# Attention scores through four single PSUM banks, row maxima through one double and one single bank

## The chip, the cores and the metric

The kernel runs on one core of a Trainium2 chip. The metric is the device time of one execution in microseconds (us). The kernel before took 948.18 us, the median of three runs (947.07 to 959.93). The profiled execution took 946.91 us, of which 945.1 us are its span.

## The reference

A transformer block with conditioning, on x of 2 x 1024 x 288 in float32. What the change touches is the attention of 16 heads of 18 columns:

```python
h = _modulate(_ln(x), sh_msa, sc_msa)
qkv = (h @ w_qkv + b_qkv).reshape(B, N, 3, nh, hd).transpose(2, 0, 3, 1, 4)
q, k, v = (qkv[0], qkv[1], qkv[2])
attn = jax.nn.softmax(jnp.einsum('bhqd,bhkd->bhqk', q, k) * hd ** (-0.5), axis=-1)
o = jnp.einsum('bhqk,bhkd->bhqd', attn, v).transpose(0, 2, 1, 3).reshape(B, N, C)
o = o @ w_proj + b_proj
x = x + g_msa[:, None, :] * o
```

Ahead of it stand the layer norm and the projections, behind it a second layer norm, a choice of two of four experts for each token, and the experts' two matrix products.

## The kernel before

The program has four stages: a setup (to about 81 us of the span), the attention (to about 523 us), a stage between (output projection, second norm, gate, loading of the experts' weights), and the experts (from about 631 us).

The attention works on 8 groups (`GG`), each of 4 heads (`GH`) of one batch. A group has 16 steps: two halves of 512 queries, each with 8 tiles of 128 keys. A step makes, for each of the 4 heads, the scores of 128 keys against 512 queries (`scores`, L1165), their exponentials on ScalarE (`exponential`, L1033), and adds their product with v to a bank `o_ps` (`values`, L1179). The values of a step are issued one step later.

The maximum of each query's scores is needed ahead of the exponentials. So every score is computed twice. Beside the steps of one group TensorE computes, for a later half, the scores with queries along the partitions (`maxima`, L1132), and VectorE reduces them to row maxima (L1064). Such a product of 128 queries by 512 keys is called a block. A half of a group (a "turn") has 32 blocks. When a turn's blocks are done, VectorE reduces them to one row each (`rowmax`, L1068), TensorE transposes those ("rows", L1139), VectorE splits the result in two parts (L1078, L1080), and two DMAs put them in the operand of the later scores. When a half's values are done, ScalarE copies `o_ps` to `o_sb` (L1040), TensorE transposes that ("out", L1145), and VectorE normalises it (L1087, L1091).

Maxima, rows and out are *items* with one running number n. Item n uses the buffer `m_ps[n % 2]`; a max item of before fills both banks of it with two blocks, and one reduction of 1024 elements per partition reads them. Before TensorE starts item n it waits for `max_free` n + 1, a count that begins at 2 and that VectorE raises once for each item it has finished. So item n starts when item n-2 is finished. In `MaxPlan` it is written which items are issued in which step: 48 blocks (`AHEAD`) ahead of the first step (the *lead*), then 4 a step (`RATE`), until all 512 are done in the middle of the eighth group.

The order on TensorE in a step is fixed: the scores of heads 0 and 1; the step's first item; the values of the step before; the scores of heads 2 and 3; its second item; in the steps 1, 4, 7 and 10 of the first six groups half of a projection for a later group (`project`, L441, 7 matmuls); any further items; the rest of the projection.

Scores and projections share a ring of single banks `s_ps` (`S_BANKS`): the k-th user takes bank k modulo the number of banks, and waits until ScalarE has read the one that many places back (`slot_free`). Two heads' operands lie on partitions 0 to 55 and 64 to 119, so that two matmuls next to each other, of an even and an odd head, use different halves of the array's rows. Blocks too alternate between an even and an odd head.

All eight PSUM banks are in use: 3 in the ring, 4 for the maxima, 1 for `o_ps`.

Of the kernel before, what the change touches and what calls it, by code (L numbers as in the profile page):

```python
# [6 lines left out]
ALU = mybir.AluOpType  # L7
ACT = mybir.ActivationFunctionType
AX = mybir.AxisListType
# [6 lines left out]
P = 128  # L16
# [10 lines left out]
HALF = N // 2  # L27
# [25 lines left out]
def f32(ap):  # L53

    return ap.bitcast(F32)
# [38 lines left out]
def build_kernel(nc, x, cond, w_adaln, b_adaln, w_qkv, b_qkv, w_proj, b_proj, w_gate, w1, b1, w2, b2, out):  # L94
# [20 lines left out]
    with outer:  # L115
# [20 lines left out]
        with before_experts:  # L136
            mod_late = far(before_experts, "mod_late", [P, B, 3 * C])
            outputs_in = OutputTiles(far, sem, before_experts, o_dram)
            setup_and_attention = ExitStack()
            with setup_and_attention:  # L140
                v_aug = sb(setup_and_attention, "v_aug", [P, NT, NH, HA])

                wqk = (sb(setup_and_attention, "wqk_raw", [P, 3, 2, GC]),
                       sb(setup_and_attention, "wqk_hi", [P, 3, 2, GH, HP], F32R),
                       sb(setup_and_attention, "wqk_lo", [P, 2, 2, GH, HP], F32R),
                       sb(setup_and_attention, "bqk", [P, GG, 2]),
                       sem(setup_and_attention, "w_ld"), sem(setup_and_attention, "w_split"),
                       sem(setup_and_attention, "bias_ld"))
                heads = HeadParts(nc, sb, sem, setup_and_attention, x_hi, x_lo, wqk)
                late.stage_in(heads.parts)  # L150
                setup(nc, sb, pb, sem, xt, cond, w_adaln, b_adaln, w_qkv, b_qkv, x_hi, x_lo, mod_late, g_mlp, ident,
                      half_neg, v_aug, wqk, heads, outputs_in.tiles)
                attention(nc, sb, pb, sem, w_qkv, ident, v_aug, wqk, heads, o_dram, late, outputs_in)
            gate_bank = pb(outer, "gate_bank", [P, 512])
            between(nc, sb, pb, sem, xt, ot, outputs_in, mod_late, ident, half_neg, xn_dram, gate_bank, logits, late, x1_st)
# [640 lines left out]
PAIRS = GH // 2  # L796
BLOCKS = 2 * GH * QT
PAIR_BLOCKS = 2
S_BANKS = 3
AHEAD = 48  # L800
RATE = 4
PROJ_AT = (1, 4, 7, 10)
# [9 lines left out]
def proj_item(g, u):  # L812

    return u if g == 1 else score_item(g - 2, PROJ_AT[u], GH - 1) + 1


class MaxPlan:
# [22 lines left out]

    def maxima(self, items, upto):
        while self.block < min(upto, 2 * GG * BLOCKS):
            n = PAIR_BLOCKS
            if self.block + n > upto:
                break
            items.append((self.count, "max", self.block // BLOCKS, self.block % BLOCKS, n))
            self.block, self.count = self.block + n, self.count + 1
# [7 lines left out]
def attention(nc, sb, pb, sem, w_qkv, ident, v_aug, wqk, heads, o_dram, late, outputs_in):  # L855
# [7 lines left out]
    ctx = ExitStack()  # L863
    with ctx:
# [4 lines left out]
        negmax = sb(ctx, "negmax", [P, 2, BLOCKS])  # L869
# [8 lines left out]
        late.tail_buffers(sb, ctx)  # L878

        s_ps = [pb(ctx, f"s_ps{i}", [P, HALF]) for i in range(S_BANKS)]  # L880
        m_ps = [pb(ctx, f"m_ps{i}", [P, 2, HALF]) for i in range(2)]
        o_ps = pb(ctx, "o_ps", [P, HALF])

        zero_ok = sem(ctx, "zero_ok")
# [15 lines left out]
        def max_bank(n):  # L900

            return m_ps[n % 2][:, 0]
# [76 lines left out]
        def _(pool):  # L979
# [8 lines left out]
            def parts(g, u):  # L988
                half, a = u // 2, u % 2
                hi, lo = ((heads.Q_HI, heads.Q_LO), (heads.K_HI, heads.K_LO))[a]  # L990
                pool.wait_ge(slot_free, S_BANKS + proj_item(g, u) + 1)
                if u == 0:
# [24 lines left out]
        def _(act):  # L1017

            act.sem_inc(slot_free, S_BANKS)

            def project(g, u):
                k = proj_item(g, u)
                act.wait_ge(slot_mm, k + 1)
                act.wait_ge(parts_ok, heads.parts_count(g, u) - 4)
                nc.scalar.activation(heads.proj_f[:, u % 2], s_ps[k % S_BANKS][:], ACT.Identity,  # L1025
                                     bias=wqk[3][:, g, u % 2:u % 2 + 1]).then_inc(slot_free, 1)

            def exponential(g, st, h):
                k = score_item(g, st, h)
                act.wait_ge(slot_mm, k + 1)  # L1030
                if h == 0:
                    act.wait_ge(pv_free, 16 * g + st + 1)
                nc.scalar.activation(probs[:, st % 2, h], s_ps[k % S_BANKS][:], ACT.Exp, scale=SCALE)\  # L1033
                  .then_inc(slot_free, 1)
# [21 lines left out]
        @block.vector  # L1056
        def _(dve):
            nc.vector.memset(o_ps[:], 0.0).then_inc(zero_ok, 1)
            dve.sem_inc(max_free, 2)

            def maxima(n, turn, first, count):
                half = turn % 2
                dve.wait_ge(max_mm, n + 1)
                nc.vector.tensor_reduce(negmax[:, half, first:first + count], m_ps[n % 2][:], AX.X, ALU.max, negate=True)\  # L1064
                  .then_inc(max_free, 1)
                if first + count == BLOCKS:
                    dve.wait_ge(max_free, 2 + n + 1)
                    nc.vector.tensor_reduce(rowmax[:, half].rearrange("p (h b) -> p b h", h=2),  # L1068
                                            negmax[:, half].rearrange("p (b k h) -> p b h k", k=2, h=2), AX.X, ALU.min)\
                      .then_inc(rowmax_ok, 1)  # L1070

            def rows(n, turn):
                g, half = turn // 2, turn % 2
                bank = max_bank(n)
                dve.wait_ge(max_mm, n + 1)
                if g >= 1:
                    dve.wait_ge(rows_ld[half], 64 * g)
                nc.vector.tensor_copy(rows_hi[:, half], bank[0:GH * QT, 0:P]).then_inc(rows_step, 1)  # L1078
                dve.wait_ge(rows_step, turn + 1)
                nc.vector.tensor_tensor(rows_lo[:, half], bank[0:GH * QT, 0:P], f32(rows_hi[:, half]),  # L1080
                                        ALU.subtract).then_inc(max_free, 1)

            def normalise(n, turn):
                g, half = turn // 2, turn % 2
                o = max_bank(n).rearrange("p (t c) -> p t c", c=HP)
                dve.wait_ge(max_mm, n + 1)
                nc.vector.reciprocal(rsum[:, half], o[:, :, HD]).then_inc(rsum_ok, 1)  # L1087
                dve.wait_ge(rsum_ok, turn + 1)
                if g >= 1:
                    dve.wait_ge(out_st[half], 16 * g)  # L1090
                nc.vector.tensor_tensor(o_norm[:, half], o[:, :, 0:HD],  # L1091
                                        rsum[:, half].unsqueeze(2).broadcast_to([P, QT * GH, HD]),
                                        ALU.mult).then_inc(max_free, 1)

            def item(n, kind, turn, first, count):
                if kind == "max":
                    maxima(n, turn, first, count)
                elif kind == "rows":
                    rows(n, turn)
                else:  # L1100
                    normalise(n, turn)

            for items in (plan.lead, *plan.steps, plan.last):
                for it in items:
                    item(*it)

        @block.tensor
        def _(pe):
            pe.sem_inc(pv_free, 2)

            def project(g, u, some):
                k = proj_item(g, u)
                if some.start == 0:
                    if u == 0:
                        pe.wait_ge(w_split, 4 * (g + 1))
                    pe.wait_ge(slot_free, k + 1)
                mm = heads.products(g, u % 2, u // 2, s_ps[k % S_BANKS][:], some)
                if some.stop == len(PRODUCTS):
# [30 lines left out]
            def item(n, kind, turn, first, count):  # L1149
                if kind == "max":  # L1150
                    maxima(n, turn, first, count)
                elif kind == "rows":
                    rows(n, turn)
                else:
                    outputs(n, turn)
# [892 lines left out]
```

## Time and profile before

| what | value |
|---|---|
| median of 3 runs | 948.18 us |
| profiled execution, and its span | 946.91 us, 945.1 us |
| TensorE busy / VectorE busy / ScalarE busy | 827.9 / 568.5 / 476.4 us |
| attention, first to last values | 114.49 to about 523 us |
| lead, first block to first scores | 82.40 to 110.89 us |

A line of the page or of a table of groups gives the program line, the engine, the operation, output and inputs with their shapes, and how many; then the busy time and the mean of one, and the idle time of the engine just ahead with what ended it. In a timeline the first number is the start in us from the span's start, the second the length of the merged instructions, and in brackets stands the idle time ahead. The ends of matmuls are modelled, so the starts are what to read.

### The profile page before, as it was taken

What the parts mean: (1) busy time and instruction counts of PE and PEld (TensorE: products, weight loads), DVE (VectorE), ACT (ScalarE), POOL (GpSimd) and SP (SyncE); (2) the same over time, 40 slices, a digit from 0 to 9 for tenths busy, and PEclk for the clock granted to TensorE, in tenths of its full rate; (3) what the DMA queues carried; (4) which work ended last, traced back from release to release, by engine and by line L of the source; (5) the groups of instructions that cost most, each with busy time, mean ns of one, the idle gap of its engine ahead of it and who ended that gap; (6) DMA issues with size and microseconds to landing.
All of it is one profiled execution on the core that took longest, in us unless ns stands there. A gap on an engine that the chain in (4) does not pass through costs nothing. (4 is left out here: it accounts for less than half of the span.)

```text
span 945.1 us, 15242 instructions
## 1 busy us (share of the span) xinstructions
PE 827.9 (88%) x5111; PEld 554.2 (59%) x5111; DVE 568.5 (60%) x994; ACT 476.4 (50%) x975; POOL 341.3 (36%) x348
## 2 busy tenths in 40 slices
PE   4886799999999999999988885369999999999995
PEld 3683333333333333333322563259999999999995
DVE  3765878777787778778860493825455434434432
ACT  0540267666676676667777364344334333333331
POOL 6534221131212222110422298066555444344332
PEclk9896799999999999999999795579999999999998
DMA  8021120424131221203222394134332222222221
GB/s 219 10 57 28 40 49 20 88 83 92 22 85 23 63 51 34 65 8 84 78 55 66 110 285 153 53 109 113 81 64 36 39 46 37 38 45 38 38 37 20
DMA packets 56384, 62.98 MB, mean 67 GB/s; under 512 B 24184, under 2 KB 50662, under 8 KB 55736
## 3 DMA queue, kind: packets, MB, share of 16 engines
q1 hardware_dynamic: 47304, 49.30, 20.1%
q0 software_dynamic: 8400, 12.12, 7.7%
q8 instruction: 46, 0.75, 0.3%
q10 hardware_dynamic: 608, 0.59, 0.2%
q14 instruction: 26, 0.21, 0.1%
HBM read 33.87 MB, written 15.73 MB: 52 GB/s over the span
## 5 line engine op out<-in xcount | busy, mean ns | idle before, releaser
L1064 DVE TENSOR_REDUCE negmax<-m_ps 128x2 f32<-128x1024 f32 x256 | 306.5, 1221 | 73.9 <-PE m_ps L1132 73.7
L1033 ACT ACTIVATE probs<-s_ps 128x512 f32<-128x512 f32 x512 | 269.8, 602 | 105.3 <-PE s_ps L1165 105.2
L1165 PE MATMUL s_ps<-stack 56*128 56x512 f32 x512 | 161.5, 476 | 21.2 <-ACT probs L1033 21.2
L1165 PEld LDWEIGHTS s_ps<-stack 56*128 56x128 f32 x512 | 65.5, 185 | 181.8 <-ACT probs L1033 154.6
L1132 PE MATMUL m_ps<-stack 54*128 54x512 f32 x512 | 136.6, 452 | 15.2 <-DVE negmax L1064 7.9
L1179 PE MATMUL o_ps<-probs,v_aug 128*19 128x512 f32 x1024 | 136.4, 605 | 6.3 <-ACT o_sb L1040 5.1
L2013 PE MATMUL gate_bank<-weights,ht_hi 128*128 x630 | 127.1, 296 | 0.4 <-DVE ht_lo L1909 0.4
L1989 PE MATMUL h_ps<-weights,xt_hi 128*128 x525 | 115.3, 350 | 4.6 <-DVE xt_hi L1902 4.6
L995 POOL CAST parts<-proj_f 128x512 fp32r<-128x512 f32 x28 | 17.1, 610 | 261.9 <-ACT proj_f L1025 129.3
L1687 POOL DMA_INDIRECT out<-res,ido x35 | 56.9, 1624 | 140.5 <-DVE res L1931 140.5
L1735 ACT CAST ht_hi<-ht_ps 128x384 fp32r<-128x384 f32 x105 | 43.6, 488 | 119.7 <-PE ht_ps L2000 119.7
L2013 PEld LDWEIGHTS gate_bank<-weights,ht_hi 128*128 128x128 f32 x630 | 101.4, 189 | 0.6 <-issue 0.6
L1989 PEld LDWEIGHTS h_ps<-weights,xt_hi 128*128 128x128 f32 x525 | 93.9, 193 | 5.2 <-issue 5.2
L2013 PE MATMUL gate_bank<-weights,ht_lo 128*128 x315 | 93.2, 296 | 0.0
L1729 ACT ACTIVATE hid<-h_ps 128x384 f32<-128x384 f32 x105 | 51.5, 492 | 69.5 <-PE h_ps L1989 69.3
L1132 PEld LDWEIGHTS m_ps<-stack 54*128 54x128 f32 x512 | 56.7, 192 | 34.9 <-DVE negmax L1064 15.4
L1931 DVE SCALAR_TENSOR_TENSOR res<-gate_bank,cws,scale 128x288 f32<-128x288 f32 x35 | 18.1, 518 | 93.5 <-PE gate_bank L2013 91.6
L1901 DVE TENSOR_TENSOR xt_lo<-tx_ps,xt_hi 128x256 fp32r<-128x256 f32 x35 | 14.9, 425 | 82.6 <-issue 58.6
L2013 PEld LDWEIGHTS gate_bank<-weights,ht_lo 128*128 128x128 f32 x315 | 59.2, 188 | 0.0
L1909 DVE TENSOR_TENSOR ht_lo<-ht_ps,ht_hi 128x384 fp32r<-128x384 f32 x105 | 52.1, 551 | 5.4 <-ACT ht_hi L1735 5.1
L1989 PE MATMUL h_ps<-weights,xt_lo 128*128 x210 | 54.8, 342 | 0.0
L1025 ACT ACTIVATE proj_f<-s_ps,bqk 128x512 f32<-128x512 f32 x28 | 19.3, 688 | 63.7 <-PE s_ps L441 63.7
(213 smaller groups left out, 1117.9 us busy)
## 6 DMA issues: line engine op xcount, KB each, us to landing
stack<-parts SPq DMA_DIRECT2D x96, 144.0 KB
w_raw<-in_L_cond_w SPq DMA_DIRECT2D x9, 432.0 KB
w_raw<-in_L_cond_w SPq DMA_DIRECT2D x9, 384.0 KB
xn_scratch<-h SPq DMA_DIRECT2D x16, 192.0 KB, 3.7
x_in<-in_x SPq DMA_DIRECT2D x4, 576.0 KB, 8.6
o_scratch<-o_norm SPq DMA_DIRECT2D x16, 144.0 KB, 2.4
o_in<-o_scratch SPq DMA_DIRECT2D x16, 144.0 KB, 2.6
xr<-in_x SPq DMA_DIRECT2D x16, 144.0 KB, 3.0
```

Source lines behind the costliest of these rows:

```text
L1025: nc.scalar.activation(heads.proj_f[:, u % 2], s_ps[k % S_BANKS][:], ACT.Identity, bias=wqk[3][:, g, u % 2:u % 2 + 1]).then_inc(slot_free, 1)
L1033: nc.scalar.activation(probs[:, st % 2, h], s_ps[k % S_BANKS][:], ACT.Exp, scale=SCALE)\
L1064: nc.vector.tensor_reduce(negmax[:, half, first:first + count], m_ps[n % 2][:], AX.X, ALU.max, negate=True)\
L1132: mm = nc.tensor.matmul(m_ps[n % 2][:, i], stack[s][r, j, 0, half, qt * P:(qt + 1) * P], stack[s][r, j, 1, kh], start=True, stop=True)
L1165: nc.tensor.matmul(s_ps[k % S_BANKS][:], stack[s][r, j, 1, kt // QT, (kt % QT) * P:(kt % QT + 1) * P], stack[s][r, j, 0, half], start=True ...
L1179: mm = nc.tensor.matmul(o_ps[h * HP:h * HP + HA], v_aug[:, tile, (g % NG) * GH + h], probs[:, st % 2, h], start=(kt == 0), stop=(kt == KT ...
L1687: nc.gpsimd.indirect_dma_start(out_rows, bass.IndirectOffsetOnAxis(ap=ido[:, j:j + 1], axis=0), res[j % 2][:], None, compute_op=ALU.add).t ...
L1729: nc.scalar.activation(hid[:, c * UPC:(c + 1) * UPC], h_ps[c][:, 0:UPC], ACT.Gelu_apprx_tanh)\
L1735: nc.scalar.copy(ht_hi[:, 3 * c:3 * (c + 1)], ht_ps[c][:]).then_inc(hthi_ok, 1)
L1909: nc.vector.tensor_tensor(ht_lo[:, s], ht_ps[c][:], f32(ht_hi[:, s]), ALU.subtract)\
L1989: mm = nc.tensor.matmul(h_ps[c][:, 0:UPC], (xt_hi, xt_lo)[xs][:, xk], words(j, (3 * ws + wk) * H + c * UPC, UPC), start=(i == 0), stop=(i ...
L2013: mm = nc.tensor.matmul(y_ps[:, 0:C], hs[:, ht], words(j, 5 * H + (HT * ws + ht) * C, C), start=False, stop=(ht == HT - 1 and i == 2))
```

## The change

The ring `s_ps` has four banks. The second buffer of the maxima has one bank. A max item with an even number has two blocks, one with an odd number has one, and the last block of a turn goes alone where only one is left. Everything else (the number of blocks in each step as far as they fit, the order within a step, the matmuls) is written as it was.

```diff
-S_BANKS = 3
+S_BANKS = 4
@@ def maxima(self, items, upto):
         while self.block < min(upto, 2 * GG * BLOCKS):
-            n = PAIR_BLOCKS
+            room = BLOCKS - self.block % BLOCKS
+            n = PAIR_BLOCKS if self.count % 2 == 0 and room >= PAIR_BLOCKS else 1
             if self.block + n > upto:
                 break
@@ def attention
-        m_ps = [pb(ctx, f"m_ps{i}", [P, 2, HALF]) for i in range(2)]
+        m_ps = [pb(ctx, f"m_ps{i}", [P, 2 - i, HALF]) for i in range(2)]
@@ VectorE, def maxima
-                nc.vector.tensor_reduce(negmax[:, half, first:first + count], m_ps[n % 2][:], AX.X, ALU.max, negate=True)\
+                nc.vector.tensor_reduce(negmax[:, half, first:first + count], m_ps[n % 2][:, 0:count], AX.X, ALU.max, negate=True)\
```

In all there are 162 double and 188 single max items where there were 256 double ones. D is a double and S a single in what follows.

The first place is TensorE's queue in a plain step (no projection, rows or out). Before, one item stands on each side of the values (L1179), always in the other buffer:

```order
L1179 MATMUL o_ps<-probs,v_aug 19x512 x4
L1165 MATMUL s_ps1<-stack0 128x512
L1165 MATMUL s_ps2<-stack0 128x512
L1132 MATMUL m_ps1<-stack0 128x512 x2
L1165 MATMUL s_ps0<-stack0 128x512
L1165 MATMUL s_ps1<-stack0 128x512
L1132 MATMUL m_ps0<-stack0 128x512 x2
L1179 MATMUL o_ps<-probs,v_aug 19x512 x4
```

Now (the lines are one further down) the steps differ in turn. One such step, and the beginning of the next:

```order
L1180 MATMUL o_ps<-probs,v_aug 19x512 x4
L1166 MATMUL s_ps0<-stack0 128x512
L1166 MATMUL s_ps1<-stack0 128x512
L1133 MATMUL m_ps0<-stack1 128x512 x2
L1133 MATMUL m_ps1<-stack1 128x512
L1166 MATMUL s_ps2<-stack0 128x512
L1166 MATMUL s_ps3<-stack0 128x512
L1133 MATMUL m_ps0<-stack1 128x512 x2
L1180 MATMUL o_ps<-probs,v_aug 19x512 x4
L1166 MATMUL s_ps0<-stack0 128x512
L1166 MATMUL s_ps1<-stack0 128x512
L1133 MATMUL m_ps1<-stack1 128x512
```

Between the two lines L1180 the double buffer `m_ps0` is filled twice with a single in between; before, no buffer was filled twice between two values.

The second place is TensorE's queue around the rows item, in a step with a projection. Before:

```order
L1165 MATMUL s_ps2<-stack0 128x512
L1165 MATMUL s_ps0<-stack0 128x512
L1139 MATMUL m_ps0<-ident,rowmax 16x128
L441 MATMUL s_ps1<-stretch,wqk_hi 128x512 x3
L441 MATMUL s_ps1<-stretch,wqk_lo 128x512
L1132 MATMUL m_ps1<-stack1 128x512 x2
L441 MATMUL s_ps1<-stretch,wqk_lo 128x512
L441 MATMUL s_ps1<-stretch,wqk_hi 128x512 x2
L1165 MATMUL s_ps2<-stack0 128x512
L1165 MATMUL s_ps0<-stack0 128x512
L1132 MATMUL m_ps0<-stack1 128x512 x2
L1179 MATMUL o_ps<-probs,v_aug 19x512 x4
```

Now:

```order
L1166 MATMUL s_ps3<-stack0 128x512
L1166 MATMUL s_ps0<-stack0 128x512
L1140 MATMUL m_ps0<-ident,rowmax 16x128
L441 MATMUL s_ps1<-stretch,wqk_hi 128x512 x3
L441 MATMUL s_ps1<-stretch,wqk_lo 128x512
L1133 MATMUL m_ps1<-stack1 128x512
L1133 MATMUL m_ps0<-stack1 128x512 x2
L441 MATMUL s_ps1<-stretch,wqk_lo 128x512
L441 MATMUL s_ps1<-stretch,wqk_hi 128x512 x2
L1166 MATMUL s_ps2<-stack0 128x512
L1166 MATMUL s_ps3<-stack0 128x512
L1133 MATMUL m_ps1<-stack1 128x512
```

Two items became three: a single stands ahead of the double, and one behind the scores.

The third place is the end of the lead on TensorE, up to the first scores. Before, every item was a double:

```order
L1132 MATMUL m_ps1<-stack0 128x512 x2
L1132 MATMUL m_ps0<-stack0 128x512 x2
L1132 MATMUL m_ps1<-stack0 128x512 x2
L1132 MATMUL m_ps0<-stack0 128x512 x2
L1165 MATMUL s_ps1<-stack0 128x512
L1165 MATMUL s_ps2<-stack0 128x512
```

Now:

```order
L1133 MATMUL m_ps0<-stack0 128x512 x2
L1133 MATMUL m_ps1<-stack0 128x512
L1133 MATMUL m_ps0<-stack0 128x512 x2
L1133 MATMUL m_ps1<-stack0 128x512
L1166 MATMUL s_ps0<-stack0 128x512
L1166 MATMUL s_ps1<-stack0 128x512
```

The lead has 24 doubles before, and now 16 doubles and 15 singles for 47 blocks.

## Rows read from the trace of the kernel before

**Rows 1.** The page, busy time: us (share of the span) x instructions.

```profile
PE 827.9 (88%) x5111; PEld 554.2 (59%) x5111; DVE 568.5 (60%) x994; ACT 476.4 (50%) x975; POOL 341.3 (36%) x348
```

**Rows 2.** The page, costliest groups: the maxima's reductions, the exponentials, the scores' weight loads.

```profile
L1064 DVE TENSOR_REDUCE negmax<-m_ps 128x2 f32<-128x1024 f32 x256 | 306.5, 1221 | 73.9 <-PE m_ps L1132 73.7
L1033 ACT ACTIVATE probs<-s_ps 128x512 f32<-128x512 f32 x512 | 269.8, 602 | 105.3 <-PE s_ps L1165 105.2
L1165 PEld LDWEIGHTS s_ps<-stack 56*128 56x128 f32 x512 | 65.5, 185 | 181.8 <-ACT probs L1033 154.6
```

**Rows 3.** Windows of a group and of three plain steps: busy by engine, PEclk, DMA, GB/s.

```profile
220.53:273.55 53.02, 50.05 (x294) 19.82 (x295) 41.14 (x43) 36.85 (x71) 10.95 (x14) 1.00 0.24 52
261.83:270.33 8.50, 7.85 (x51) 2.75 (x49) 7.62 (x7) 6.20 (x13) 0.28 (x1) 1.00 0.25 55
```

**Rows 4.** Timeline of TensorE, one plain step.

```profile
212.63 0.50 PE L1165 MATMUL s_ps<-stack 56*128 56x512 f32 x2
212.96 0.39 PE L1132 MATMUL m_ps<-stack 54*128 54x512 f32 x2
213.20 0.39 PE L1165 MATMUL s_ps<-stack 56*128 56x512 f32 x1
213.81 0.50 PE L1165 MATMUL s_ps<-stack 56*128 56x512 f32 x1 [0.23 <-ACT probs L1033]
213.81 0.73 PE L1132 MATMUL m_ps<-stack 54*128 54x512 f32 x2
214.47 1.05 PE L1179 MATMUL o_ps<-probs,v_aug 128*19 128x512 f32 x8
215.46 0.50 PE L1165 MATMUL s_ps<-stack 56*128 56x512 f32 x2
```

**Rows 5.** Timelines of ScalarE and VectorE, the same step.

```profile
213.16 2.06 ACT L1033 ACTIVATE probs<-s_ps 128x512 f32<-128x512 f32 x4 [0.76 <-PE s_ps L1165]
...
213.40 2.40 DVE L1064 TENSOR_REDUCE negmax<-m_ps 128x2 f32<-128x1024 f32 x2 [0.43 <-PE m_ps L1132]
```

**Rows 6.** Timeline of TensorE, a step without maxima near the attention's end.

```profile
510.10 0.73 PE L1165 MATMUL s_ps<-stack 56*128 56x512 f32 x3
511.28 0.50 PE L1165 MATMUL s_ps<-stack 56*128 56x512 f32 x1 [0.45 <-ACT probs L1033]
511.76 1.05 PE L1179 MATMUL o_ps<-probs,v_aug 128*19 128x512 f32 x8
512.75 0.50 PE L1165 MATMUL s_ps<-stack 56*128 56x512 f32 x2
```

**Rows 7.** Timelines of TensorE and VectorE, an out item and what waits for it.

```profile
227.58 0.50 PE L1132 MATMUL m_ps<-stack 54*128 54x512 f32 x2 [0.18 <-DVE o_norm L1091]
228.01 1.05 PE L1179 MATMUL o_ps<-probs,v_aug 128*19 128x512 f32 x8
...
227.06 0.46 DVE L1091 TENSOR_TENSOR o_norm<-m_ps,rsum 128x288 f32<-128x288 f32 x1
```

**Rows 8.** Timeline of TensorE, starts of values in the third group.

```profile
220.53 1.05 PE L1179 MATMUL o_ps<-probs,v_aug 128*19 128x512 f32 x8 [0.33 <-ACT o_sb L1040]
224.67 1.05 PE L1179 MATMUL o_ps<-probs,v_aug 128*19 128x512 f32 x8
...
230.83 1.05 PE L1179 MATMUL o_ps<-probs,v_aug 128*19 128x512 f32 x8
...
235.38 1.05 PE L1179 MATMUL o_ps<-probs,v_aug 128*19 128x512 f32 x8
...
245.18 1.05 PE L1179 MATMUL o_ps<-probs,v_aug 128*19 128x512 f32 x8
248.40 1.05 PE L1179 MATMUL o_ps<-probs,v_aug 128*19 128x512 f32 x8 [0.33 <-ACT o_sb L1040]
```

**Rows 9.** Timeline of VectorE in the lead.

```profile
93.13 3.49 DVE L1064 TENSOR_REDUCE negmax<-m_ps 128x2 f32<-128x1024 f32 x3 [0.58 <-PE m_ps L1132]
97.24 4.62 DVE L1064 TENSOR_REDUCE negmax<-m_ps 128x2 f32<-128x1024 f32 x4 [0.62 <-PE m_ps L1132]
101.89 0.19 DVE L1068 TENSOR_REDUCE rowmax<-negmax 128x16 f32<-128x32 f32 x1
...
103.36 12.53 DVE L1064 TENSOR_REDUCE negmax<-m_ps 128x2 f32<-128x1024 f32 x11
```

**Rows 10.** Timeline of TensorE in the lead, and its window (columns as in Rows 3).

```profile
102.52 1.55 PE L1132 MATMUL m_ps<-stack 54*128 54x512 f32 x4
...
81.00:114.50 33.50, 24.39 (x82) 12.17 (x81) 26.96 (x26) 5.61 (x10) 9.68 (x12) 0.70 0.10 20
```

## The prediction

> **What bounds the kernel now.** I began with the busy times: TensorE 88% of the span, VectorE 60%, ScalarE 50% [rows 1]. In a group in the middle of the attention, 53.02 us for 16 steps, TensorE is busy 50.05, VectorE 41.14 and ScalarE 36.85 [rows 3]. Modelled matmul ends fill gaps, so the question of who waits for whom goes to the groups: the scores' weight loads sat idle 154.6 us for the exponentials, and the reductions 73.7 us for TensorE [rows 2]. No engine is full; the steps are a loop with two handovers.
>
> The timeline of a plain step [rows 4, 5] shows the loop. It lasts 2.83 us (212.63 to 215.46). The second score of the next pair starts at 213.81, late by a wait for ScalarE: the ring has three banks, and it needs the one whose exponential began at 213.16 and took 0.60 [rows 2]. Behind it in the queue stand a double and the values, which start 0.66 later at 214.47. After the values, 0.98 later, come the next scores. So with three banks the loop is: score to exponential 0.53, exponential 0.60, handover 0.05, score and double 0.66, values 0.98, in sum 2.83.
>
> Where no maxima are left a step takes 2.65 us (510.10 to 512.75) [rows 6]. There the second score still waits for its bank, and the values start at 511.76, 1.66 behind the scores, once two exponentials are done; that part does not depend on the ring. So 2.65 is the floor of a step with any ring.
>
> **The fourth bank.** It takes away the wait at 213.81. A plain step can come down from 2.83 to 2.65, by 0.18, if nothing else is late. TensorE's own work in it is four pairs of 0.33 and the values of 0.98, or 2.3 us [rows 4], so TensorE has room. A step with a projection takes 4.14 (220.53 to 224.67) [rows 8], with the seven matmuls packed and no ring wait in it: nothing is gained there.
>
> **The maxima, plain steps.** The double item has 1.22 us of VectorE [rows 2]. For the single I take the line between that (1024 elements) and the small reduction of 32 elements in 0.19 [rows 9]: 1.03/992 = 1.04 ns per element, so 0.69 us for 512. Behind another of its kind a double starts 1.14 after it (12.53/11) [rows 9], 0.08 before the first ends; so a queued single costs about 0.61. The work per three plain steps is four doubles and four singles, 4 x 1.14 + 4 x 0.61 = 7.0, against 6 x 1.14 = 6.8 before, of 8.5 us. VectorE isn't full by this. What decides is the wait of a double for the double two items back.
>
> From here on 0 is the start of values. The scores come at 0.98, an item behind them at 1.32 (0.98 + 0.34), its reduction 0.44 later (212.96 to 213.40) [rows 4, 5]. A stalled item starts 0.06 after its release (227.52 to 227.58), and values behind a stalled double come 0.43 later (228.01) [rows 7]. Three kinds of step follow each other:
> - A, with D and S behind the values and D ahead of the next: the first D is reduced from 1.76 to 2.98. TensorE reaches the next D at 1.32 + 3 x 0.33 = 2.31, but may start it only at 3.04. Values at 3.47. Before: 2.83, so +0.64.
> - B, with S and D behind and S ahead of the next: S reduced from 1.76 to 2.45, the next S at 2.51, values at 2.84: 0.
> - C, with S behind and D ahead of the next: the D before was done at about 1.3, so values come at the floor, 2.65: -0.18.
> In sum a cycle of three costs 8.96 instead of 8.49. The ring's gain is left in one step of three, and A pays for it several times.
>
> **The other steps.** At a change of half the values also wait for the copy of `o_ps`, and the step has 3.22 (245.18 to 248.40) [rows 8]; two a group are of kind A and go to 3.47: +0.25 each. The out item in a step without projection: its normalisation starts behind one more single, and the double that waits for it starts near 3.2 instead of 2.91; +0.30. Out with a projection: one more array slot of 0.33 less 0.10 of a wait that the new single covers: +0.23. Rows without projection: D waits for the split rows until 2.39, then 0.43, scores 0.34, S 0.33: 3.49 instead of 2.84, +0.65. Rows with projection, 4.55 (230.83 to 235.38) [rows 8]: one more slot, +0.33. The projection in step 7 gets a double in its middle, as the one with rows has (4.55 against 4.14), and one single more: +0.61. Step 1: 0.
>
> For a group with projections: two A 1.28, two at the changes 0.50, three C -0.54, three B 0, out 0.30 and 0.23, rows 0.65 and 0.33, step 7 0.61: +3.36. Six groups: +20.2. The seventh, without projections, has a C more, two outs of 0.30 and two rows of 0.65: +3.0. In the eighth three steps are left: +0.1. Behind them no step has maxima, and they stay at 2.65.
>
> **The lead.** VectorE goes through doubles back to back at 1.14 and sets the time [rows 9]. Now a double can follow the double before only after 1.22 + 0.06 + the way through TensorE. That way is 0.54 at the full clock (the idle 0.58 and 0.62 of rows 9 hold it), and 0.84 at the lower one (102.52 to 103.36) [rows 9, 10], where the mean clock of the lead was 0.70 [rows 10]. So three blocks take 1.82 to 2.12 us instead of 1.5 x 1.14 = 1.71. In the first 32 blocks every second group of three items between projections gets shorter by 0.7, but only 18 blocks instead of 24 are done with the projections, and six more come after them at 0.6 each: about +2.2. The 15 behind the rows, at 2.12 for three, take 10.6 instead of 8 x 1.14 = 9.1: +1.5, and 0.3 for the wait at the join. I take +4; from below 0 (work alone) and from above 7 (all at the lower clock).
>
> At the attention's end all is in series with the stages behind; they keep their length.
>
> **A rule against the rows.** The step's waits show VectorE busy 7.62 of 8.50 us in plain steps [rows 3], with an idle 0.43 at each turn [rows 5]. The Trainium skill, Perfetto Trace Analysis, section Optimizing Scalar/DVE Operations, says that where such an engine isn't saturated but makes bubbles elsewhere, breaking up instructions may let work finish sooner. By that rule the split would pay, and the time would be that of the first rival below. In the rows no bubble of before comes from the length of a reduction outside the lead, so I give the rule little.
>
> A single also uses half of the array's rows with no partner: the last max matmul in 213.81 to 214.47 starts 0.33 after its partner in time [rows 4], as much as a pair. I count a single at 0.33. If it could run beside its neighbour, step 7, rows and outs would be 0.2 to 0.3 cheaper: -1 us a group. The Trainium skill, TensorE: Matmul & The Clock Gate, Part 3, The mechanism, says that weight loads overlap running matmuls only when the row group differs; by it a single between unlike halves could be hidden, and the sum would be some 6 us lower.
>
> **Sum.** 20.2 + 3.0 + 0.1 + 4 = 27 us on the profiled 946.9: 974. The median of the runs is 1.3 above the profiled time: 975. As plain error I see the singles (-6), the lead (-4 to +3), and 0.1 of a microsecond in each A and rows step (5 a group: 4 in all).
>
> **Rivals.**
> 1. *The ring pays, the maxima don't stall* (8%). If the second D of kind A were free when TensorE gets there (at 2.31), all 66 plain steps would drop by 0.18: -12 us, and with the lead 936 to 940, not slower. For it: the wait for ScalarE is the one that the trace names most [rows 2]. Against: it needs the reduction of 1.22 to end 0.7 earlier. The place is the third item of an A step, and it decides from a release at about 2.3.
> 2. *Half and half* (16%): TensorE's stall is partly given back, since the exponentials run ahead in it, or singles are cheap. A at 3.1 and rows at 3.1 give some +1.2 a group: 950 to 962.
> 3. *The clock* (10%). In the lead the granted clock was 0.70 [rows 10] after TensorE had waited, in the steps 1.00 [rows 3]. If the longer waits keep the whole lead and some first steps at 1.2 GHz, the lead costs 6 to 10 more and the first steps too: 982 to 995.
> 4. My forecast (66%): 962 to 984.
>
> Two per cent, about what can be told from no change here, are 19 us: 967. The forecast's part above that is about nine tenths: slower 0.66 x 0.9 + 0.10 = 0.69, same 0.29, faster 0.02. The range from 954 to 986 leaves out the first rival, a part of the second and most of the third.
>
> **What would show it.** In the trace of the changed kernel: plain steps in a cycle of 3.47, 2.84 and 2.65; in the first of them TensorE's double waits for VectorE's reduction by 0.6 to 0.7; no wait of the second score for its bank; a single reduction of 0.69; a group of 56.4 us instead of 53.0; the first scores at about 115 instead of 110.9; steps without maxima at 2.65. If all plain steps take 2.65 to 2.8, the sum is wrong at A; if a single costs less than 0.2 on TensorE, at the projections; if the lead's clock is another, at the lead.

## The result

The changed kernel takes 986.6 us, the median of four runs (982.33 to 990.75), against 947.63 before in the same comparison: a ratio of 1.0379, 95% interval 1.0282 to 1.0476. It is slower. The forecast was 975, and the median lies 0.6 above the upper end of the range; the ratio times the 948.18 that the forecast started from is 984.1, inside it. The profiled execution is the shortest of the four, 982.33 us with a span of 980.5, which is 35.4 longer than before.

The page of the changed kernel, busy times:

```profile
PE 833.1 (85%) x5111; PEld 559.0 (57%) x5111; DVE 575.6 (59%) x1088; ACT 477.5 (49%) x975; POOL 342.1 (35%) x348
```

It answers to [rows 1]: no engine has noticeably more work. The groups of the changed kernel (each reads busy time and mean of one, then the idle time ahead):

```profile
L1133 PE MATMUL m_ps<-stack 54*128 54x512 f32 x512 | 149.4, 458 | 50.2 <-DVE negmax L1065 42.3
...
L1166 PEld LDWEIGHTS s_ps<-stack 56*128 56x128 f32 x512 | 59.7, 191 | 125.9 <-ACT probs L1034 95.9
```

The scores' wait for ScalarE fell from 154.6 us [rows 2] to 95.9, as a fourth bank should do: with the ring back at three banks it is 145.6 (first experiment below). In its place TensorE's max matmuls wait 42.3 us for VectorE's reductions, where they waited 7.9:

```profile
L1132 PE MATMUL m_ps<-stack 54*128 54x512 f32 x512 | 136.6, 452 | 15.2 <-DVE negmax L1064 7.9
```

The groups by shape show the price of the two kinds:

```profile
L1065 DVE TENSOR_REDUCE negmax<-m_ps 128x2 f32<-128x1024 f32 x162 | 197.9, 1222 | 45.5 <-PE m_ps L1133 45.3
L1065 DVE TENSOR_REDUCE negmax<-m_ps 128x1 f32<-128x512 f32 x188 | 129.0, 686 | 53.6 <-PE m_ps L1133 53.6
```

The single takes 0.686 us; the estimate was 0.69.

The timeline of TensorE through three plain steps of the third group, the three kinds in a row:

```profile
276.32 1.05 PE L1180 MATMUL o_ps<-probs,v_aug 128*19 128x512 f32 x8
277.31 0.50 PE L1166 MATMUL s_ps<-stack 56*128 56x512 f32 x2
277.65 0.40 PE L1133 MATMUL m_ps<-stack 54*128 54x512 f32 x2
277.88 0.39 PE L1166 MATMUL s_ps<-stack 56*128 56x512 f32 x1
277.89 0.39 PE L1133 MATMUL m_ps<-stack 54*128 54x512 f32 x1
278.12 0.39 PE L1166 MATMUL s_ps<-stack 56*128 56x512 f32 x1
279.37 0.50 PE L1133 MATMUL m_ps<-stack 54*128 54x512 f32 x2 [0.86 <-DVE negmax L1065]
279.81 1.05 PE L1180 MATMUL o_ps<-probs,v_aug 128*19 128x512 f32 x8
...
282.46 1.05 PE L1180 MATMUL o_ps<-probs,v_aug 128*19 128x512 f32 x8 [0.46 <-ACT probs L1034]
...
284.96 0.50 PE L1133 MATMUL m_ps<-stack 54*128 54x512 f32 x1 [0.31 <-DVE negmax L1065]
285.39 0.63 PE L1180 MATMUL o_ps<-probs,v_aug 128*19 128x512 f32 x4
```

From values to values: 3.49 (kind A), 2.65 (C), 2.93 (B). Before, each had 2.83 [rows 4]. VectorE over the same time:

```profile
278.09 3.05 DVE L1065 TENSOR_REDUCE negmax<-m_ps 128x2 f32<-128x1024 f32 x3 [0.43 <-PE m_ps L1133]
281.56 1.82 DVE L1065 TENSOR_REDUCE negmax<-m_ps 128x1 f32<-128x512 f32 x2 [0.42 <-PE m_ps L1133]
```

The first double begins at 278.09 and takes 1.22, to 279.31; the next double on TensorE starts at 279.37. Its neighbours, both scores, had started by 278.12: with four banks they wait for nothing, and TensorE then stands idle behind a double.

Windows of the changed kernel (columns as in Rows 3): a whole group, the last group's steps around its last rows item, and behind it.

```profile
232.38:288.86 56.48, 50.21 (x296) 20.56 (x294) 42.19 (x55) 36.96 (x72) 10.99 (x14) 1.00 0.22 49
508.51:518.89 10.38, 7.94 (x53) 3.07 (x52) 8.31 (x12) 6.91 (x14) 1.51 (x1) 1.00 0.05 14
518.89:541.53 22.64, 18.35 (x77) 4.52 (x76) 0.56 (x2) 12.18 (x24) 5.79 (x4) 0.53 0.13 41
```

A group takes 56.48 instead of 53.02 [rows 3]; 56.4 was forecast. The third row was not: in the first steps without maxima the granted clock was 0.53 (0.50 from 520.1 to 544.0), and a plain one of them lasts 3.81 us instead of 2.65 [rows 6]. Before, the corresponding stretch ran at the full clock up to 522.0, and at 0.50 for the 1.2 us that were left to the last values:

```profile
489.50:523.00 33.50, 26.79 (x151) 7.59 (x154) 1.27 (x4) 24.29 (x47) 5.81 (x4) 0.98 0.17 50
```

The lead on VectorE goes as worked out, a double and a single in 1.82 and 0.30 idle behind them, 2.12 for three blocks:

```profile
105.43 1.82 DVE L1065 TENSOR_REDUCE negmax<-m_ps 128x2 f32<-128x1024 f32 x2
107.55 1.82 DVE L1065 TENSOR_REDUCE negmax<-m_ps 128x2 f32<-128x1024 f32 x2 [0.29 <-PE m_ps L1133]
```

The 35.4 us of span, by the starts of values: up to the first values 4.4 (118.87 against 114.49); the first group 4.0; the next five 3.5 each, 17.5; the seventh 2.9; the last, to the start of its last matmul of values, 7.0 (50.55 against 43.53); everything behind it -0.4. Below, the length of the last group is taken to the first matmul of its last values: 50.1 here, 42.7 before.

### The profile page after: what moved, and what is told of

Read it like the earlier page. It is cut to its first block and busy times, and to the rows that moved or that the text cites. A ratio compares the mean times of both kernels' runs of the same rounds, so it can differ in the third digit from the quotient of the medians.

```text
span 980.5 us, 15336 instructions
## 1 busy us (share of the span) xinstructions
PE 833.1 (85%) x5111; PEld 559.0 (57%) x5111; DVE 575.6 (59%) x1088; ACT 477.5 (49%) x975; POOL 342.1 (35%) x348
## 5 line engine op out<-in xcount | busy, mean ns | idle before, releaser
L1065 DVE TENSOR_REDUCE negmax<-m_ps 128x2 f32<-128x1024 f32 (+1 forms) x350 | 317.0, 934 | 99.0 <-PE m_ps L1133 98.8
L1133 PE MATMUL m_ps<-stack 54*128 54x512 f32 x512 | 149.4, 458 | 50.2 <-DVE negmax L1065 42.3
L1180 PE MATMUL o_ps<-probs,v_aug 128*19 128x512 f32 x1024 | 141.0, 624 | 21.3 <-ACT probs L1034 20.0
L1166 PE MATMUL s_ps<-stack 56*128 56x512 f32 x512 | 133.5, 472 | 0.0
L1166 PEld LDWEIGHTS s_ps<-stack 56*128 56x128 f32 x512 | 59.7, 191 | 125.9 <-ACT probs L1034 95.9
L1133 PEld LDWEIGHTS m_ps<-stack 54*128 54x128 f32 x512 | 71.0, 192 | 103.5 <-DVE negmax L1065 80.4
L1180 PEld LDWEIGHTS o_ps<-probs,v_aug 128*19 128x19 f32 x1024 | 17.5, 98 | 64.0 <-ACT probs L1034 38.6
```

Source lines behind the costliest of these rows:

```text
L1133: mm = nc.tensor.matmul(m_ps[n % 2][:, i], stack[s][r, j, 0, half, qt * P:(qt + 1) * P], stack[s][r, j, 1, kh], start=True, stop=True)
L1166: nc.tensor.matmul(s_ps[k % S_BANKS][:], stack[s][r, j, 1, kt // QT, (kt % QT) * P:(kt % QT + 1) * P], stack[s][r, j, 0, half], start=True ...
L1180: mm = nc.tensor.matmul(o_ps[h * HP:h * HP + HA], v_aug[:, tile, (g % NG) * GH + h], probs[:, st % 2, h], start=(kt == 0), stop=(kt == KT ...
```

## The experiments

All times are medians, and each ratio is against the kernel before, run beside it on the same chip. The comparisons among variants rest on these ratios and on the traces.

**The ring back to three banks.**

```diff
-S_BANKS = 4
+S_BANKS = 3
```

> The changed kernel with the ring put back to three banks (one PSUM bank is left unused). My theory: the fourth bank only helps the plain steps of the short kind (single behind the values, double ahead of the next), which go from 2.65 back to 2.83 us; the steps of 3.47 and 2.92 keep their length, a group takes 57.0 instead of 56.5, and the kernel is 3 to 5 us slower than the changed one. Rival, the fourth bank is worth its 0.18 in every plain step: over 10 us slower than the changed one.

Measured: 991.9 us, ratio 1.0475 (1.0458 to 1.0493); a group 57.0. Plain steps 3.48, 2.93 and 2.84. The short one on TensorE:

```profile
284.41 1.05 PE L1180 MATMUL o_ps<-probs,v_aug 128*19 128x512 f32 x8
285.39 0.50 PE L1166 MATMUL s_ps<-stack 56*128 56x512 f32 x2
285.73 0.39 PE L1133 MATMUL m_ps<-stack 54*128 54x512 f32 x1
285.97 0.40 PE L1166 MATMUL s_ps<-stack 56*128 56x512 f32 x1
286.58 0.49 PE L1166 MATMUL s_ps<-stack 56*128 56x512 f32 x1 [0.21 <-ACT probs L1034]
286.58 0.72 PE L1133 MATMUL m_ps<-stack 54*128 54x512 f32 x2
287.24 0.63 PE L1180 MATMUL o_ps<-probs,v_aug 128*19 128x512 f32 x4
```

The second score waits again, with a double behind it, as in [rows 4]. At the full clock that is the whole worth of the fourth bank here: 0.18 us in one plain step of three, 0.5 a group. Against the changed kernel the medians differ by 5 us, the two profiled spans by 9.8 (990.3 against 980.5; the changed kernel's was its shortest). Of the 9.8, the first seven groups hold 4.3, the last group 2.9 (53.0 instead of 50.1; at the lower clock a plain step takes 4.05 instead of 3.81), 2.9 stand ahead of the first values, and -0.3 behind the last. The other two kinds did not feel the ring. So the rival falls by the steps in the trace; the times alone would not decide it, since the ratios differ by 0.0096, or 9 us.

**The first item ahead of the scores, in the kernel before.**

```diff
-                    scores(g, st, 0)
-                    for it in items[:1]:
-                        item(*it)
+                    early = t > 0 and all(it[1] == "max" for it in plan.steps[t - 1])
+                    for it in items[:1] if early else []:
+                        item(*it)
+                    scores(g, st, 0)
+                    for it in items[:1] if not early else []:
+                        item(*it)
```

> The kernel before with one edit on TensorE: a step's first max item is issued ahead of its first two scores instead of behind them, except where the step before holds a rows or out item. My theory of the loop (score, two exponentials, values) says that the ring wait is only harmful because a double stands behind it; moved ahead of it, the wait for the bank runs beside the second exponential and a plain step takes 2.65 instead of 2.83 with three banks. Nine steps a group: about 51.4 instead of 53.0, the kernel at 935 to 939. Rival, the fourth bank is what such a step needs: no change, 2.83.

Measured: 940.49 us, ratio 0.994 (0.9923 to 0.9957); a group 51.6. TensorE in a plain step:

```profile
261.22 1.05 PE L1179 MATMUL o_ps<-probs,v_aug 128*19 128x512 f32 x8
262.20 0.50 PE L1165 MATMUL s_ps<-stack 56*128 56x512 f32 x2
262.54 0.69 PE L1132 MATMUL m_ps<-stack 54*128 54x512 f32 x4
263.08 0.81 PE L1165 MATMUL s_ps<-stack 56*128 56x512 f32 x2
263.88 0.62 PE L1179 MATMUL o_ps<-probs,v_aug 128*19 128x512 f32 x4
```

The step takes 2.66 with three banks. The wait for the bank is still there (the fourth score starts at 263.39, 0.05 behind the end of the exponential that held its bank), but no max item stands between it and the values any more. Eight steps a group with 0.17 make the 1.4 us between 53.0 and 51.6; the ninth plain step, the one with rows and no projection, stayed at 2.83. The kernel got less than forecast (935 to 939), for two more reasons that the trace shows: the last group took 45.0 instead of 42.7, because the clock fell there (two steps of 4.05 and 3.81), and the first step after the lead took 6.05 instead of 4.72.

**The double's reduction cut to half its elements.**

```diff
-                nc.vector.tensor_reduce(negmax[:, half, first:first + count], m_ps[n % 2][:, 0:count], AX.X, ALU.max, negate=True)\
+                nc.vector.tensor_reduce(negmax[:, half, first:first + count], m_ps[n % 2][:, 0:count, 0:HALF // count], AX.X, ALU.max, negate=True)\
```

This kernel leaves half of the keys out of its maxima.

> The changed kernel, but a double's reduction reads only the first half of each of its two banks, so the maxima leave out half of the keys there: 512 elements, about 0.69 us instead of 1.22. TensorE's work and order are the same. Theory: a step of 3.47 is the way over the double's reduction and comes down by 0.53 to about 2.95; 2.65 and 2.92 stay; a group takes 54.5 to 55. Over seven groups and the lead 15 to 20 us faster than the changed kernel, but still no faster than the one before. Rival, TensorE's singles are what the steps pay for: under 5 us.

Measured: 966.16 us, ratio 1.019 (1.0169 to 1.0212); a group 54.9; the step of 3.47 takes 2.95, the other two stay at 2.66 and 2.93, and the changes of half go back to 3.23. TensorE and VectorE in the long step:

```profile
268.88 1.05 PE L1180 MATMUL o_ps<-probs,v_aug 128*19 128x512 f32 x8
...
271.40 0.50 PE L1133 MATMUL m_ps<-stack 54*128 54x512 f32 x2 [0.32 <-DVE negmax L1065]
271.83 0.63 PE L1180 MATMUL o_ps<-probs,v_aug 128*19 128x512 f32 x4
```

```profile
270.65 1.98 DVE L1065 TENSOR_REDUCE negmax<-m_ps 128x2 f32<-128x512 f32 x3 [0.95 <-PE m_ps L1133]
```

TensorE's matmuls are the same, the release comes 0.53 earlier, and so do the values. The long step is the way over that one reduction. The median is 20 us below the changed kernel's, the ratio by 0.0189, or 18 us, and the profiled span by 16.0. Of these the seven groups hold 9.4 and the lead 5.0; 4.0 more are the last group's, because the clock fell later in it (24.6 us behind the last rows item instead of 1.4), and behind the attention 2.3 were lost. Yet the kernel is slower than before: steps of 2.93, and the steps with rows, out and projections, still wait for a single or carry one more item.

**Three single banks in turn.**

```diff
-        m_ps = [pb(ctx, f"m_ps{i}", [P, 2 - i, HALF]) for i in range(2)]
+        m_ps = [pb(ctx, f"m_ps{i}", [P, 1, HALF]) for i in range(M_BANKS)]
```

with M_BANKS = 3, every item one block, and item n in bank n modulo 3.

> The changed kernel (ring of four) with its three banks for the maxima used as three single banks in turn, item n waiting for item n-3, one block in each. Theory, that the wait for the item that last had the buffer makes the long steps: a step has one block ahead of the values and three behind; the one ahead waits only for a single reduced from 1.76 to 2.45, so each plain step takes 2.84 to 2.95, none 3.47, and a group 54 to 55. VectorE has 4 x 0.61 a step instead of 2 x 1.14. The kernel is 10 to 15 us faster than the changed one, still slower than the one before. Rival, the number of small items itself costs (350 before, 512 now): slower than the changed one.

Measured: 985.55 us, ratio 1.041 (1.0385 to 1.0436); a group 56.5. The plain steps came as expected, all 2.93 and none of 3.47:

```profile
280.98 1.05 PE L1181 MATMUL o_ps<-probs,v_aug 128*19 128x512 f32 x8
...
283.48 0.49 PE L1134 MATMUL m_ps<-stack 54*128 54x512 f32 x1 [0.32 <-DVE negmax L1066]
283.90 0.63 PE L1181 MATMUL o_ps<-probs,v_aug 128*19 128x512 f32 x4
```

The group and the kernel did not: I had 54 to 55 and 10 to 15 us less than the changed one. I had only looked at plain steps. Against the changed kernel the long steps give back 0.55 each and the changes of half 0.25, but the short ones go from 2.65 to 2.93, and step 1 has three blocks beside its projection where a single stood (4.77 instead of 4.12); in a group these cancel. The profiled kernel lost 3.8 more in the first group (60.9 instead of 57.0), where the granted clock stayed at 0.50 until 130.9, against 120.7 in the changed one. So both sayings were half right: the long step is the wait for the buffer, and small items cost where TensorE is packed. Three banks for the maxima are too few either way.

**Matmuls in the wait for the last row maxima, and in the steps without maxima.** Three kernels from the changed one. The first adds these lines to the rows item, ahead of its wait for `rowmax_ok`:

```diff
+                if turn == 2 * GG - 1:
+                    for i in range(8):
+                        nc.tensor.matmul(max_bank(n), stack[0][0:heads.MAX_ROW, 0, 0, 0, 0:P], stack[0][0:heads.MAX_ROW, 0, 1, 0],
+                                         start=True, stop=True)
```

> The changed kernel with eight added matmuls of 512 columns (1.8 us) into the bank of the last rows item, in the wait of 2 us for its row maxima; their result is overwritten. Theory: the granted clock fell to half for 24 us after that wait, and the steps of 3.81 us in the last group are 2.65 at the full clock. If the idle time of TensorE there brings the fall, it does not come, and the kernel is about 8 us faster than the changed one (972 to 976). Rival, the long steps come from elsewhere or the clock falls anyway in the steps without maxima: no change, 980 to 991.

Measured: 987.32 us, ratio 1.0425 (1.0399 to 1.045). The windows:

```profile
518.89:530.00 11.11, 8.30 (x53) 2.88 (x53) 1.78 (x4) 7.22 (x15) 0.65 (x1) 1.00 0.27 83
530.00:545.00 15.00, 11.81 (x60) 3.26 (x56) 0.71 (x2) 8.75 (x17) 5.14 (x4) 0.66 0.18 47
545.00:561.00 16.00, 11.45 (x54) 2.37 (x54) 0.00 (x0) 9.35 (x18) 0.00 (x0) 0.62 0.01 3
```

The fall at 520 did not come, and the plain steps there took 2.65. But two others came behind it, at 531.7 for 10.2 us and at 548.7, and nothing was gained. The wait alone isn't the cause.

The second has two such matmuls at each of the two places for items, in the steps behind the last rows item:

```diff
+            def fill(t, n=2):
+                if t > rows_step_at:
+                    pe.wait_ge(max_free, 2 + plan.rows_at[2 * GG - 1] + 1)
+                    for i in range(n):
+                        r = slice(0, heads.MAX_ROW)
+                        nc.tensor.matmul(max_bank(plan.rows_at[2 * GG - 1]), stack[(GG - 1) % heads.STACKS][r, 0, 0, 0, 0:P],
+                                         stack[(GG - 1) % heads.STACKS][r, 0, 1, 0], start=True, stop=True)
```

> The changed kernel with two added matmuls of 512 columns at each of the two places for max items, in the steps behind the last rows item, where there are no maxima; their results are not used. Theory: the steps of 3.8 us come from the clock, which falls while TensorE has little to do in these steps. With the places filled it should stay at 1.00 up to the attention's end apart from the fall that follows the wait at the last rows item, and the kernel be 0 to 8 us faster than the changed one. Rival, the added work only lengthens the steps (2.65 has room for 4 x 0.23): slower.

Measured: 980.46 us, ratio 1.0354 (1.0335 to 1.0372). In its trace the clock still falls at 520, for 10 us instead of 24, and does not fall again before the attention's end; the last group takes 47.5 instead of 50.1. The third has both:

> The changed kernel with both additions, the eight matmuls in the last rows item's wait (e3_fill_wait, where the fall of the clock at 520 us was gone but one came at 532 and one at 549) and those in the steps without maxima (e6_fill_steps, where the fall at 520 stayed, with 10 us instead of 24, and no other came). Theory: each takes away the fall that it took away alone; no fall is left before the attention's end, the last group takes 43.5 to 44.5 us instead of 50.1, and the kernel about 6 us less than the changed one, 975 to 981. Rival, the falls come at set times whatever TensorE does: a fall between 515 and 560, 980 or more.

Measured: 977.78 us, ratio 1.0308 (1.0292 to 1.0323). The windows of the last group:

```profile
513.90:524.90 11.00, 10.01 (x61) 4.46 (x59) 8.33 (x12) 6.93 (x14) 1.69 (x1) 1.00 0.05 13
524.91:558.00 33.09, 31.35 (x191) 13.58 (x190) 1.27 (x4) 24.26 (x47) 5.82 (x4) 1.00 0.17 51
```

No fall is left ahead of the attention's end; the last group takes 44.2 and its plain steps without maxima 2.66. (The profiled execution itself, 986.04 us, had a longer stretch at the lower clock in the lead; five of seven runs were between 976.7 and 979.2.) The intervals of the ratios of the changed kernel and of this one overlap, because the changed kernel's runs scatter by 8 us; so the gain in the kernel's time is not told apart, and what is shown is the last group in one trace each: 50.1 against 44.2.

**The same in the reordered kernel.** Three variants of the kernel with the first item ahead of the scores: the matmuls in the steps without maxima; these with two ahead of each later max item of the lead, eight in the wait for the first row maxima and four in the wait for the last; the first with the four in the last rows item's wait alone. The edit in the lead:

```diff
+                if i > 12 and it[1] == "max":
+                    pe.wait_ge(slot_free, S_BANKS + 2)
+                    for j in range(2):
+                        r = slice(0, heads.MAX_ROW)
+                        nc.tensor.matmul(s_ps[UNITS % S_BANKS][:], stack[0][r, 0, 0, 0, 0:P], stack[0][r, 0, 1, 0],
+                                         start=True, stop=True)
```

> The kernel before with the first max item ahead of the scores (as in e2_item_first) and the same added matmuls in the steps without maxima. In e2_item_first the clock fell 14 us before the attention's end and two steps took 4.05 and 3.81 instead of 2.65. If low activity of TensorE brings that, it stays at 1.00 here and the kernel takes 935 to 938 instead of 940.5. Rival: the fall comes anyway, 940 or more.

> e7_first_fill with added matmuls in the lead too: two of 512 columns ahead of each max item after the last projection, eight in the wait for the first row maxima, four in the wait for the last. Theory: the clock in the lead falls after TensorE waits for VectorE; filled, it stays at 1.00, the first steps of the attention keep their 4.1 and 2.65 us and the kernel gains 2 to 4 us on e7_first_fill. Rival: at the lower clock the fillers (0.46 each) take longer than the 1.14 us of a reduction leave, and the lead gets 3 to 8 us longer.

> e7_first_fill (the kernel before with the first max item ahead of the scores, and added matmuls in the steps without maxima), with four matmuls in the last rows item's wait, where a fall of 3 us was left. Theory: no fall before the attention's end, the last group takes 43.1 as in e8_lead_fill instead of 44.6, and the kernel 1 to 2 us less than e7_first_fill, 937 to 939. Rival: nothing measurable.

Measured: 940.21 us, 0.9925 (0.9902 to 0.9947); 942.24 us, 0.9958 (0.9935 to 0.9981); 942.47 us, 0.9936 (0.9917 to 0.9954). The long fall ahead of the attention's end is gone in all three, and the last group takes 44.6, 43.1 and 43.1 instead of 45.0. The kernels aren't faster by it beyond their intervals. In the lead the added matmuls did harm: the first scores come 38.8 us after the first block instead of 35.9, and the first step is 0.5 shorter. (The first block of the attention is the one that starts at 75.7 here, at 73.8 in the plain reordering and at 73.24 in the kernel before; at 82.40, as the table of the kernel before has it, its lead is well under way.) All four of these kernels beat the kernel before by 0.4 to 0.8%, and the plain reordering gives all that can be told apart.

## Why the prediction was right, and what it missed

- *The loop* (score, two exponentials, values: 2.65; with a late score and a double behind it 2.83): right. The steps of kind C take 2.65 with four banks and 2.84 with three, and the reordering gets 2.66 with three.
- *Kind A at 3.47*: right, 3.47 to 3.48 in all groups. Halving the reduction took off the 0.53 that it should.
- *Kind B at 2.84*: 2.92 to 2.93. The mis-sized term is a stalled single: 0.43 (284.96 to 285.39) where I had taken 0.33, though the stalled double of [rows 7] with its 0.43 was the nearer row.
- *A group*: +3.5 for +3.4. The terms, measured against forecast: out without projection +0.24 (+0.30), rows with projection +0.23 (+0.33), rows without +0.56 (+0.65), step 7 +0.63 (+0.61), out with projection +0.27 (+0.23), changes +0.25 (+0.25). That the sum fits so well is in part luck: the three steps of kind B cost 0.3 more than the nothing they were given, the steps with rows, out and projections 0.2 less, and the two nearly cancel.
- *A single at 0.33*: beside a score it cost less. In the step of kind A above it starts at 277.89, within 0.01 of the score at 277.88, and the next score follows at 278.12. TensorE could so have reached the second double about 2.03 behind the values (278.12 and 0.24 more) instead of 2.31, which changes nothing there, since its reduction ended 2.99 behind them. Out, rows and step 7 together, without the changes of half, cost 1.93 a group instead of 2.12: 0.2 less, and not the 1 that the other reading of a single would have given.
- *The lead*: +4.4 to the first values for +4, with the 2.12 us for three blocks; and 0.9 more in the first step. One reading was off without effect: in a row of eleven, doubles start 1.13 apart, (12.53 - 1.22)/10, and not 1.14.
- *A rule against the rows*: the rows held. Breaking up the reductions gave VectorE's results no earlier where it mattered, and the double that stayed double became the wait. The split came with one bank fewer for the maxima; no run here splits the reductions and keeps four.
- *What failed* is the sentence "behind them no step has maxima, and they stay at 2.65". Six of them took 3.8 to 4.4 us each, since the clock was at its lower level, 1.2 GHz, for 24 us: 7.0 us in the last group for +0.1. With the fall avoided the last group takes 44.2, so that 5.9 of the loss go by it, and up to 1.5 stay for which +0.1 was given (the step with the last rows item alone takes 4.15 instead of 3.56). My rival on the clock had it in the lead and the first steps, and the trace shows it at the other end. With the fall avoided the kernel comes to 977.8, near the 975 forecast.
- *The median over the profiled time*: I added 1.3; it is 4.3 (986.6 against 982.3). The four runs of the changed kernel took 982.3, 984.6, 988.6 and 990.8 us at mean granted clocks of 0.929, 0.927, 0.919 and 0.917: the lower the clock, the longer the run.

## What to carry to other kernels

Buffers that alternate in size don't average: the wait is set by the largest item and by how often its buffer comes up between two fixed points of the producer's queue, so look where one buffer is needed twice in that stretch, and price it as release plus handover plus what stands behind. Before giving a bank to a ring that waits, ask what is queued behind the waiting instruction; moving it ahead of the wait brought here eight of nine plain steps to 2.66 us, against the 2.65 that a fourth bank gives at best, and it took no bank. When a change makes TensorE wait, price the clock behind the wait too, not only the wait.

## What the runs showed of the hardware

The granted clock fell from 2.4 to 1.2 GHz in the steps without maxima, in which TensorE has only four score matmuls and the values to do in 2.65 us. In the changed kernel it fell 1.4 us behind the last rows item, in the kernel before 32.7 us behind it, just ahead of the attention's end. At the last rows item TensorE had stood still for 0.69 us before and for 1.76 in the changed kernel:

```profile
489.23 0.27 PE L1139 MATMUL m_ps<-ident,rowmax 128*16 128x128 f32 x1 [0.69 <-DVE rowmax L1068]
...
518.69 0.27 PE L1140 MATMUL m_ps<-ident,rowmax 128*16 128x128 f32 x1 [1.76 <-DVE rowmax L1069]
518.89 1.05 PE L1180 MATMUL o_ps<-probs,v_aug 128*19 128x512 f32 x8
```

The same in every profile (one execution each; us, counted from the last rows item):

| kernel | TensorE idle ahead of it | clock falls behind it | for | last values |
|---|---|---|---|---|
| before | 0.69 | 32.7 | 13.7 | 34.0 |
| changed | 1.76 | 1.4 | 23.9 | 40.4 |
| ring of three | 1.29 | 0.4 | 27.3 | 43.0 |
| half reduction | 1.22 | 24.6 | 27.3 | 36.9 |
| three singles | 1.84 | 0.6 | 23.9 | 40.4 |
| changed, wait filled | 0 | 10.8 and 27.9 | 10.2 and 30.7 | 40.4 |
| changed, steps filled | 1.76 | 1.2 | 10.2 | 37.8 |
| changed, both filled | 0 | none before the end | | 33.8 |
| reordered | 1.64 | 27.5 | 20.5 | 36.5 |
| reordered, steps filled | 1.64 | 0.3 | 3.4 | 35.7 |
| reordered, both filled (and the lead too) | 0.25 (0.24) | none before the end | | 34.3 (34.3) |

Filling the wait moved the fall from 1.4 to 10.8 us behind the item, filling the steps shortened it, and only both together kept it off. So these steps and the wait ahead of them both bear on it. The length of the wait doesn't settle when it comes: after 1.64 us the clock fell at once in one of the two reordered kernels and 27.5 us later in the other, and after 1.22 and 1.29 us it fell 24.6 and 0.4 us later. What does is open; I have no run that tells it apart.

From an item that starts out of a stall to the values it is 0.42 to 0.43 us, single or double (284.96 to 285.39, 279.37 to 279.81), where it is 0.33 in a stream [rows 4].
